# Score passes of a two-attention kernel on 64-row tiles of two heads, with a ring of four PSUM banks

## The reference, cut to what matters

```python
x = L0_attn_x                                   # (4, 1024, 128)
x = x + layernorm(attention_1(layernorm(x)))    # causal, with a bias of slope[head] * (i - j)
x = x + layernorm(ffn_block(layernorm(x)))      # a second attention, not causal, then a mixture of experts

# either attention: 16 heads of 8 channels
scores = einsum('bhqd,bhkd->bhqk', q, k) * 8 ** -0.5
out    = einsum('bhqk,bhkd->bhqd', softmax(scores), v)
```

## Time and profile before

| | us |
|---|---|
| median of 3 runs | 2289.57 |
| lowest and highest | 2287.91, 2292.93 |
| span of the profiled execution | 2287.5 |

### The profile page before, as it was taken

How to read it: one execution, slowest core, us unless ns; L and a number is a source line. 1 busy time by engine, 2 the same in 40 slices (tenths; PEclk the granted TensorE clock), 3 DMA queues, 4 the chain that set the end, 5 groups by cost and what they waited for, 6 DMA issues and landing times. The chain is left out here.

```text
span 2287.5 us, 41083 instructions
## 1 busy us (share of the span) xinstructions
PE 2102.9 (92%) x11100; PEld 1223.1 (53%) x11100; DVE 1671.8 (73%) x3157; ACT 1373.5 (60%) x2647; POOL 977.3 (43%) x744
## 2 busy tenths in 40 slices
PE   5899999999999679999999999999993999999996
PEld 4455555555554534555555555555531666666664
DVE  5766667666672787777777777778822899998986
ACT  4266566666666616666666666666672655555654
POOL 3665464553610355333333333342002466565554
PEclk7799999999999679999999999999996999999998
DMA  2000000000000300000000000000001100000000
GB/s 59 1 2 1 3 1 1 2 2 1 1 1 2 110 0 1 2 1 1 2 1 1 2 1 1 1 1 1 1 1 61 51 19 19 2 19 19 19 10 10
DMA packets 27508, 24.96 MB, mean 11 GB/s; under 512 B 2409, under 2 KB 21110, under 8 KB 27282
## 3 DMA queue, kind: packets, MB, share of 16 engines
q1 hardware_dynamic: 26400, 21.91, 3.2%
q10 hardware_dynamic: 882, 0.36, 0.1%
HBM read 13.87 MB, written 6.29 MB: 9 GB/s over the span
## 5 line engine op out<-in xcount | busy, mean ns | idle before, releaser
L466 DVE TENSOR_REDUCE at_mx<-at_a 128x1 f32<-128x512 f32 (+3 forms) x1632 | 1010.8, 675 | 358.7 <-PE at_a L333 249.5
L415 ACT ACTIVATE at_probs<-at_b 128x512 f32<-128x512 f32 (+3 forms) x1792 | 888.6, 558 | 474.0 <-PE at_b L360 292.7
L333 PE MATMUL at_a<-at_km,at_fq 128*128 128x512 f32 (+1 forms) x1632 | 704.8, 439 | 20.4 <-DVE at_mx L466 9.8
L360 PE MATMUL at_b<-at_fqm,at_km 128*128 128x512 f32 (+3 forms) x1792 | 710.8, 404 | 11.4 <-ACT at_probs L415 7.6
L333 PEld LDWEIGHTS at_a<-at_km,at_fq 128*128 128x128 f32 x1632 | 316.3, 194 | 290.0 <-DVE at_mx L466 224.4
L360 PEld LDWEIGHTS at_b<-at_fqm,at_km 128*128 128x128 f32 x1792 | 339.8, 191 | 205.5 <-ACT at_probs L415 120.3
L378 PE MATMUL at_pv<-at_probs,at_vst 128*32 128x512 f32 (+3 forms) x3584 | 437.9, 561 | 1.5 <-ACT at_probs L415 1.5
L556 POOL TENSOR_TENSOR at_hi<-at_u,split_sign 128x512 fp32r<-128x512 f32 x120 | 124.9, 1041 | 441.1 <-ACT at_u L404 306.5
L1172 ACT ACTIVATE t_hid<-t_bank_h,b1t 128x512 f32<-128x512 f32 x256 | 174.3, 689 | 195.9 <-DVE t_hid_lo L1306 113.1
L1306 DVE TENSOR_TENSOR t_hid_lo<-t_hid,t_hid_hi 128x512 fp32r<-128x512 f32 x256 | 225.6, 917 | 15.0 <-ACT t_hid_hi L1179 11.8
L569 POOL TENSOR_TENSOR at_km<-at_fk,head_mask 128x2048 fp32r<-128x2048 f32 x60 | 216.1, 3602 | 11.2 <-POOL at_fk L567 11.0
(11 more groups left out here) (211 smaller groups left out, 2410.3 us busy)
## 6 DMA issues: line engine op xcount, KB each, us to landing
t_raw<-L_ffn_W SPq DMA_DIRECT2D x16, 256.0 KB, 3.1
x_first<-L_attn_x SPq DMA_DIRECT2D x4, 512.0 KB, 7.3
second_x_in<-L_attn_x SPq DMA_DIRECT2D x8, 256.0 KB, 3.1
kept<-second_joined SPq DMA_DIRECT2D x8, 256.0 KB, 2.6
kept_u<-second_normed SPq DMA_DIRECT2D x8, 256.0 KB, 2.0
t_heads_in<-tokens SPq DMA_DIRECT2D x8, 256.0 KB, 2.6
t_u_in<-kept_u SPq DMA_DIRECT2D x8, 256.0 KB, 3.1
t_x_in<-kept SPq DMA_DIRECT2D x8, 256.0 KB, 3.1
```

Of the source, the lines that this page charges most:

```text
L333: mm = pe.matmul(scores, fq[g][:, qt * P:(qt + 1) * P], km[g][:, heads[0]:heads[0] + k, kh * HALF:kh * HALF + w], start=True, stop=not dia ...
L360: mm = pe.matmul(out[:, 0:w], km[g][:, j, kt * P:(kt + 1) * P], fqm[g % 2][:, q0:q0 + w], start=True, stop=not diagonal)
L415: act.activation(probs[(t % 2) * GH + j][:, 0:w], b_bank[n % 3][:, 0:w], ACT.Exp).then_inc(exp_done, 1)
L466: dve.tensor_reduce(mx[:, kh, qt, heads[0]:heads[0] + k], a_bank[n % 3][:, 0:k * w].rearrange("p (k w) -> p k w", k=k), AX.X, ALU.max).the ...
```

## The change

- `km` holds two heads' keys for each half of the rows: head j's 32 rows lie at their own place, in plane j % 2, with zeros in the other head's rows of the same 64. A score matmul of head j uses rows 0 to 63 or 64 to 127 (`PAIR` = 64) of keys and queries. The tile is 64 x 128 of the array instead of 128 x 128.
- The heads are taken in the order 0, 2, 1, 3 in both passes, so that the row halves alternate. A first-pass chunk holds at most two heads; a causal slot has 40 chunks, 24 with a mask.
- Each mask is added by two bf16 matmuls over 64 rows of the same half (`half_ident`, `half_mask`), each carrying one half of the mask, in both passes.
- The banks of the first pass and `misc` become one ring of four (`RING`, `A_BANKS`), given out in the order of the steps "a", "proj", "otr" and "mtr"; `bank_free` waits for the reader of four places back. The second pass keeps three banks.
- The second pass runs three quads ahead instead of two, `probs` holds four quads instead of two, and "pv" of quad i + 1 stands in step i as before. In a step all "a" chunks follow the first "b"; they were spread between the four.
- Keys are no longer copied under a head mask by POOL or DVE. The last split writes `fk`, now one for each half, and SP issues four DMAs for each (32 rows x 512, 64 KB), which put the rows into `km`. First-pass matmuls wait for `keys_spread`. `km` is shared by both attentions and set to zero once by POOL in the first stage.

```diff
-                per = max(1, HALF // n)
-                per = 4 if per >= 4 else per
-                for j in range(0, GH, per):
+                per = 2 if n <= HALF // 2 else 1
+                for j in (0, 2) if per == 2 else (0, 2, 1, 3):
                     self.chunks.append((qt, kh, list(range(j, j + per)), n))
...
-        self.lead = 2
-        a_steps = nq - 4
+        self.lead = 3
+        a_steps = nq - 2 - self.lead
...
-            out += self.interleave(bs, ass)
+            out += bs[:1] + ass + bs[1:]
...
-            dp, p = (ds, q - 1) if q else (0, self.nq - 1)
+            dp, p = (0, i + 1) if i + 1 < self.nq else (1, 0)
...
-        km = [sb(f"km{i}", [P, GH, T], F32R) for i in range(4)]
-        fk = sb("fk", [P, HALF])
-        probs = [sb(f"probs{i}", [P, HALF]) for i in range(8)]
+        probs = [sb(f"probs{i}", [P, GH, HALF]) for i in range(PROBS)]
+        fk = [sb(f"fk{i}", [P, HALF], F32R) for i in range(2)]
...
-        a_bank = [bank(f"a{i}") for i in range(3)]
-        b_bank = [bank(f"b{i}") for i in range(3)]
+        a_bank = [bank(f"a{i}") for i in range(A_BANKS)]
+        b_bank = [bank(f"b{i}") for i in range(B_BANKS)]
         pv_bank = bank("pv")
-        misc = bank("misc")
...
+                def bank_free(step):
+
+                    place = places[step] - A_BANKS
+                    while True:
+                        back = 0 if place >= 0 else 1
+                        if prologue and back:
+                            return
+                        what, ds, n = held[place]
+                        if held[place] in emitted[back]:
+                            break
+                        place -= A_BANKS
+                    s = s0 + (ds - back)
+                    if what == "a":
+                        done(pe, a_read, NA, s, n)
...
-                        mm = pe.matmul(scores, fq[g][:, qt * P:(qt + 1) * P],
-                                       km[g][:, heads[0]:heads[0] + k, kh * HALF:kh * HALF + w],
+                        rows = slice(PAIR * (heads[0] // 2), PAIR * (heads[0] // 2 + 1))
+                        first = heads[0] % 2
+                        mm = pe.matmul(scores, fq[g][rows, qt * P:(qt + 1) * P],
+                                       km[g][rows, first:first + k, kh * HALF:kh * HALF + w],
                                        start=True, stop=not diagonal)
                         if diagonal:
-                            mm = pe.matmul(scores[:, :, w - P:w], ident16[:, :],
-                                           causal_mask[:, None, :].broadcast_to([P, k, P]),
-                                           start=False, stop=True)
+                            for i in range(2):
+                                mm = pe.matmul(scores[:, :, w - P:w], half_ident[rows, i, :],
+                                               half_mask[rows, i, None, :].broadcast_to([PAIR, k, P]),
+                                               start=False, stop=(i == 1))
...
-                        mm = pe.matmul(out[:, 0:w], km[g][:, j, kt * P:(kt + 1) * P],
-                                       fqm[g % 2][:, q0:q0 + w], start=True, stop=not diagonal)
-                        if diagonal:
-                            mm = pe.matmul(out[:, 0:P], causal_mask[:, :], ident16[:, :],
-                                           start=False, stop=True)
+                        out = b_bank[n % B_BANKS]
+                        rows = slice(PAIR * (j // 2), PAIR * (j // 2 + 1))
+                        mm = pe.matmul(out[:, 0:w], km[g][rows, j % 2, kt * P:(kt + 1) * P],
+                                       fqm[g % 2][rows, q0:q0 + w],
+                                       start=True, stop=(t not in plan.diagonals))
+                        if t in plan.diagonals:
+                            for i in range(2):
+                                mm = pe.matmul(out[:, 0:P], half_mask[rows, i, :], half_ident[rows, i, :],
+                                               start=False, stop=(i == 1))
...
-                        pool.tensor_tensor(km[g][:, :, half],
-                                           fk[:, None, :].broadcast_to([P, GH, HALF]),
-                                           head_mask[:, :, None].broadcast_to([P, GH, HALF]),
-                                           ALU.mult).then_inc(split_done, 1)
+                    if m:
+                        await_(keys_spread[h], KEYS, s - 1, KEYS - 1)
+                    dst = fk[h][:, :] if m else fq[g][:, half]
+                    pool.tensor_tensor(dst, part[:, :], un[:, :], ALU.add).then_inc(split_done, 1)
...
+        @block.sync
+        def _(sp):
...
+                    if ds == 3 and n == 0:
+                        done(sp, b_made, NB, s - 4, NB - 1)
+                    done(sp, split_done, 4, s, n)
+                    for j in range(GH):
+                        rows = slice(HW * j, HW * (j + 1))
+                        sp.dma_start(km[g][rows, j % 2, h * HALF:(h + 1) * HALF].bitcast(F32),
+                                     fk[h][rows, :].bitcast(F32)).then_inc(keys_spread[h], 16)
...
+                for i in range(2):
+                    pool.memset(km[i][:, :, :].bitcast(F32), 0.0).then_inc(cleared, 1)
```

More of the change, by code:

```diff
@@ L76, in __init__ @@
                 self.quads.append((qh, kt))
+        self.diagonals = [t for t, (qh, kt) in enumerate(self.quads) if causal and kt * P >= qh * HALF]
         self.na = len(self.chunks)
@@ L135, in body, with places @@
         return out
+    def places(self, steps):
+        order = [step for step in steps if step[0] in RING]
+        return {step: place for place, step in enumerate(order)}
     def prologue(self):
@@ L247, in attention @@
         dve_step = sem("dve_step")
+        keys_spread = [sem(f"keys_spread{i}") for i in range(2)]
         v_staged = sem("v_staged")
@@ L394, in _, with emit @@
                 act.sem_inc(semaphore, per)
-            def emit(steps, s0, b0, g0):
+            def emit(steps, s0, b0, g0, places, before):
                 for what, ds, n in steps:
@@ L438, in emit @@
                         un = u[n % 2]
-                        own = 5 * h if m else 5 * h + 3
+                        own = 4 * h + 2 * (n % 2)
                         done(dve, proj_read, 4, s, n)
@@ L461, in emit @@
                         if n == 0:
-                            if steps[0] == ("proj", 0, 0) and type(b0) is int and ds == 0:
+                            if places is in_prologue and ds == 0:
                                 dve.wait_ge(init, 4)
@@ L547, in emit @@
                         first = False
-                    if type(b0) is int and steps[0] == ("proj", 0, 0) and ds == 0:
+                    if places is in_prologue and ds == 0:
                         continue
@@ L552, in emit @@
                     await_(split_done, 4, s, n - 1)
-                    step = 5 * h if m else 5 * h + 3
+                    step = 4 * h + 2 * (n % 2)
                     half = slice(h * HALF, (h + 1) * HALF)
@@ L562, in emit @@
                     await_(pool_step, count, s, step + 1)
-                    if m == 0:
-                        pool.tensor_tensor(fq[g][:, half], part[:, :], un[:, :],
-                                           ALU.add).then_inc(split_done, 1)
-                    else:
-                        pool.tensor_tensor(fk[:, :], part[:, :], un[:, :], ALU.add).then_inc(pool_step, 1)
-                        await_(pool_step, count, s, step + 2)
-                        pool.tensor_tensor(km[g][:, :, half],
-                                           fk[:, None, :].broadcast_to([P, GH, HALF]),
-                                           head_mask[:, :, None].broadcast_to([P, GH, HALF]),
-                                           ALU.mult).then_inc(split_done, 1)
-            run(pool, emit)
+                    if m:
+                        await_(keys_spread[h], KEYS, s - 1, KEYS - 1)
+                    dst = fk[h][:, :] if m else fq[g][:, half]
+                    pool.tensor_tensor(dst, part[:, :], un[:, :], ALU.add).then_inc(split_done, 1)
+            run(pool, emit)
+        @block.sync
+        def _(sp):
+            for semaphore in keys_spread:
+                sp.sem_inc(semaphore, KEYS)
+            def emit(steps, s0, b0, g0, places, before):
+                for what, ds, n in steps:
+                    if what != "proj" or n % 2:
+                        continue
+                    s, h = s0 + ds, n // 2
+                    _, g = where(b0, g0, ds)
+                    if ds == 3 and n == 0:
[5 more added lines that the diff above has]
+                                     fk[h][rows, :].bitcast(F32)).then_inc(keys_spread[h], 16)
+            run(sp, emit)
 GROUPS = NT // HQ
```

130 lines of the change are left out of this document (72 added, 58 removed).

## The result

The changed kernel takes 2,216.0 us (median of 4, 2,206.6 to 2,219.4) against 2,288.7 (median of 4, 2,287.1 to 2,292.9): ratio 0.9677, 95% interval 0.9652 to 0.9702. It is faster and inside the stated range, but the gain is 73 us where 179 were forecast. The profiled execution took 2,206.6 us (span 2,204.8, against 2,287.5), so the trace shows 82.7 us of gain; the other three runs took 8 to 13 us more at a granted clock of 0.932 to 0.937 instead of 0.942. They have no trace, so those microseconds can't be placed. The profiled run of the change has 49.6 and 62.1, so it is one of the short ones in both.

What follows compares the result with a forecast made beforehand. PE was taken to bound both attentions; gains of 126 (second attention), 46 (first) and 7 us sum to 179, and 2,289.6 - 179 = 2,110 us. The stated range was 1,960 to 2,255, the forecast's own 2,040 to 2,190.

Steps and rivals of the forecast that it cites:

- What bounds the kernel before: Both attentions' steady stretches, 1,512 of 2,287.5 us: PE, busy 98 to 99% of the time, sets the pace.
- Row halves side by side: Score matmuls of both attentions: two using different 64-row halves run together, with starts in program order.
- the first rival: Score matmuls: row halves do not overlap in fp32r, items stay serial and masks cost more; about 2,415 us, chance 0.12.
- Second attention: Its steady body falls to 46.5 us, plain steps to 2.55; gain 126 us, bounds 70 to 190.
- At a projection it is not, and PE sets the step: Four projection steps per body of the second attention: PE's work sums to 3.15 us each.
- my sum of 44.9: Body of the second attention in us: 8 x 2.55 + 4 x 3.15 + 4 x 2.98.
- the 1.6: Microseconds added to the second attention's body for two nearly equal engines waiting on each other, giving 46.5.
- First attention: Causal bodies: cheaper masked items, paired unmasked ones, less new shape changes; net 2.9 us per body, 46 us.
- The third rival: Masks and same-half matmuls: a weight load waits for the matmul of its own rows; 2,250 us, chance 0.08.
- The clock: PE's granted clock in the attentions should stay at 0.97 or more, with DVE-bound steps keeping PE above 85% busy.
- the second rival: PE waits for DVE and its clock falls; with a third of attention time at 1.2 GHz, 2,440 us; chance 0.04.
- Everything else: Mainly key splitting: its masked operation leaves DVE's chain before each attention's first reduction, 9 us, less DMA delay; 7 us.

Runs made afterwards that it cites:

- the 128-row version: The changed kernel with all its score and mask matmuls on all 128 rows instead of 64, all else kept: 2,344.8 us, ratio 1.0241.

## Why the prediction was wrong, point by point

**What bounds the kernel before: right**, as the tile's 129 us show.

**Row halves side by side: right.** Two start at the same 0.01 us, and the first rival is gone. Its price was also high: the 128-row version takes 2,345 where the rival less its tile changes comes to 2,378.

**Second attention, the step that failed: "so a plain step becomes DVE's: 2.48, with a little slack 2.55".** I summed PE's work (2.25; its three terms give 2.23) and DVE's (2.48) and let the longer one set the step. A third limit was longer than both: b0 to the end of its exponential and the weights of b3 1.26 (1042.16 to 1043.42), 0.43 to the value matmuls, 0.99 for those, 2.68. All its pieces stand in the trace of before, where second-pass loads waited for exponentials for 0.8 us at most. Three banks for four blocks had been enough while PE spread the blocks and chunks over 2 us. That the halving of PE's time laid it bare, and not the new order with all chunks behind the first block, is argued; no run has the old order on the new tiles. On seven plain steps it costs only 0.15 each, 1.0 per body.

**The costlier half of the same error: "At a projection it is not, and PE sets the step: 2.25 + 0.70 + 0.20 = 3.15".** Measured 4.10. A sum of PE's work assumes that waits overlap with it. But b3 stands before the projection in the program, so the 0.43 us that PE idles for the exponential is lost first and the projection's 0.89 comes on top: 3.58 even with four chunks. The other 0.52 is the fifth chunk: the plan puts five at every projection, into a ring of four, and the fifth waits for DVE. Four such steps miss by 3.8 us. The one five-chunk step without a projection adds 0.7, transposes (3.41 on average for 2.98) 1.7. With 1.0 for the plain steps that is, rounded, the 7.3 between my sum of 44.9 and 52.2; the 1.6 that I had added for two engines waiting on each other was in that direction and too small. In total the second attention, from its first value copy to the start of its last output on ACT, went from 919.3 us (805.88 to 1725.16) to 889.6 (752.16 to 1641.77): 30 us instead of 126.

**First attention: right in sum, in part by luck.** The body takes 37.1 for 37.2. But 37.2 came from an average over 16 bodies, 40.1, less 2.9; a steady body took 40.7 before and has lost 3.6. From the first projection on ACT to the last output there the attention went from 688.3 us (51.41 to 739.75) to 637.3 (49.29 to 686.55), 51 us, of which 5 in the first body belong to "everything else": 46 as forecast. I had called it the likeliest error. A part of it was off: I priced a masked item at 0.32, hardly less than before, and took 2.5 us for unmasked pairing. The masks cost less: 0.05 per second-pass block, which leaves them worth 1.5 us where the mask's own matmul and load had been 0.13 of 0.36. Second-pass weight loads now wait for exponentials for 103 us of the stretch of the earlier trace rows (56 before), so the same chain may have taken back what cheaper masks gave; no experiment priced it in this attention. How far the two errors cancel is therefore open.

**The third rival: no.** A rule by which a weight load must wait for its own rows' matmul would have made each pair of masks pay 0.10 or more; it pays 0.05, net of waits. The page "TensorE: Matmul & The Clock Gate" (Part 3, The mechanism) of the Trainium skill says in its list of what overlaps that loads do so only where the row group differs; this trace disagrees with that sentence (the weights of a projection's second matmul, on the same 128 rows, load at 1047.16 under the first, 1047.05 to 1047.39), as the earlier trace rows did, and agrees with the one above it, by which a load may also go ahead into the background weight buffer.

**The clock: right for the steady bodies, wrong at the heads.** It is 0.98 to 0.99 in the two stretches, where it was 0.99 to 1.00. But the second rival looked only there. In the 57 us behind the second attention's first value copy it is 0.53 (65 us at 0.83 before), in the first attention's first 60 us 0.62 (0.78 before). The 128-row version has 0.87 and 0.92 in these places and is some 6 us shorter in each: 12 us that the forecast had put at nothing.

**Everything else: 6 for 7, but not resolved.** 2 us ahead of the first attention and 5 in its first body, less 1 in the first two bodies of the second. The start of the program alone varies by 6 us between traces of kernels that share its code, and the cheaper key splitting and the low clock stand in the same stretches, so the agreement shows little about either. The 64 KB transfers land in 2.0 us and no wait for them shows in the steady bodies.

What stays open: the 10 us between the profiled run and the median, what a fourth second-pass bank would give without taking it from the ring, and why the body in which the loop turns over lengthens so differently.

## What to carry to other kernels

When a change halves an engine's work, don't forecast the new period as the larger of the engines' sums: follow one buffer around its ring (write, read by the slow engine, free, next write), count how many buffers stand between two fixed points of the program order, and add to that chain everything queued behind its last wait. Then look at what the plan puts into the heaviest step, since a step with one item more than the ring has banks pays the whole wait. Here the plan, left as it was, ate almost a third of what was to be had, and a flat one gave back 32 us.

## What the runs showed of the hardware

- Two 64-row fp32r matmuls of 512 columns in different halves start at the same time (1042.16); in a mixed row of five the mean distance is 0.116 us, half of the 0.23 of the full array.
- A 128-row bf16 mask matmul of 128 columns between 64-row fp32r ones costs 0.19 us or more per block (6.1 us for 32 blocks) above a pair of 64-row masks; such a pair costs 0.05 in all. The full mask changes the tile shape and also leaves nothing beside it; the two are not told apart here, but together they cost more than a second small matmul.
- Scores and masks of two halves go on in parallel at a fine grain: five matmuls, two of them masks, start between 268.93 and 269.30.
- The granted clock can differ with the rows used, at the same program order: 0.53 with 64-row score matmuls against 0.87 with 128-row ones at the head of the second attention, although PE's rows show it busy for 50.3 of 57.3 us against 39.9 of 51.1. Matmul rows are longer at the lower clock, so the two busy shares are no measure of work.
